# Attention stage: square roots of two batches in a row, with the batches written out and a lead of two

## The reference

```
Xn = layernorm(X);  P = Xn @ W_in.T + b_in      # 16 heads of 4 x 8: Q, K, V, G
sq   = |q|^2 + |k|^2 - 2 q.k                     # 256 x 256 for each head
dist = sqrt(max(sq, 0))
W    = (1e-4 + dist) ** -2;  W = W / (1e-4 + sum(W))
A = W @ V;  O = G * A;  X + O @ W_out.T + b_out
```

## Time and profile before

| | us |
|---|---|
| median of 3 runs | 1515.87 (1515.39 to 1519.79) |
| the profiled execution | 1515.65 |
| its span, first to last instruction | 1513.9 |
| attention stage in it, first score to last update | 816.4 to 1229.7 |

### The profile page before, as it was taken

One profiled execution on the slowest core, in us unless ns is written; L12 is line 12 of the kernel. 1 busy time (PEld: TensorE's weight loads), 2 busy tenths in 40 slices (PEclk: granted clock), 3 DMA queues, 4 the chain that ended last, 5 costly groups with the idle time before them and its releaser, 6 DMA issues. The chain is left out here.

```text
span 1513.9 us, 21515 instructions
## 1 busy us (share of the span) xinstructions
PE 1302.8 (86%) x6448; PEld 636.5 (42%) x6448; DVE 1271.4 (84%) x2150; ACT 1098.4 (73%) x1594; POOL 900.4 (59%) x1054
## 2 busy tenths in 40 slices
PE   4788888998997599999997787788888579999998
PEld 3344445544553244444442233333333234444443
DVE  3999999999999988888886888888878568888885
ACT  4677877786777456556653899999999956656564
POOL 5999889989988666665665232322222026656655
PEclk8999999999999999999998677867666689999999
DMA  7122113111311043322220000000000023333331
GB/s 252 57 73 95 56 56 102 65 56 56 111 56 57 10 166 144 131 112 112 112 112 0 1 1 0 0 0 0 0 0 1 1 113 120 120 119 119 146 155 61
DMA packets 27923, 111.54 MB, mean 74 GB/s; under 512 B 4049, under 2 KB 9570, under 8 KB 19426
## 3 DMA queue, kind: packets, MB, share of 16 engines
q1 hardware_dynamic: 27010, 110.21, 19.4%
q10 hardware_dynamic: 864, 0.74, 0.2%
HBM read 108.06 MB, written 2.88 MB: 73 GB/s over the span
## 5 line engine op out<-in xcount | busy, mean ns | idle before, releaser
L1042 POOL TENSOR_TENSOR e_h_lo<-e_h,e_h_hi 128x512 f16<-128x512 f32 x272 | 314.7, 1158 | 246.4 <-ACT e_h_hi L1124 233.6
L275 POOL TENSOR_TENSOR m_h<-m_b_sb,m_dx 128x512 f32<-128x512 f32 x256 | 347.0, 1383 | 45.6 <-POOLq L67 35.8
L690 DVE TENSOR_TENSOR_SCAN m_h<-m_decay,m_h 128x1024 f32<-128x1024 f32 x112 | 255.9, 2285 | 10.9 <-DVEq L60 7.5
L393 PE MATMUL m_y_ps<-m_hc,ident 128*128 128x512 f32 x512 | 251.1, 614 | 0.0
L528 ACT ACTIVATE m_decay<-m_delta,mw_a_log 128x255 f32<-128x255 f32 x448 | 185.1, 461 | 87.7 <-DVEq L695 87.5
L1119 ACT ACTIVATE e_g<-e_g 128x512 f32<-128x512 f32 x256 | 148.9, 582 | 122.7 <-PE e_g L1064 121.5
L1124 ACT ACTIVATE e_h_hi<-e_h 128x512 f16<-128x512 f32 x272 | 169.7, 624 | 84.6 <-DVE e_h L1175 82.9
L1621 DVE TENSOR_SCALAR a_d<-a_s 128x512 f32<-128x512 f32 x256 | 170.3, 687 | 54.9 <-PE a_s L1508 35.9
L1064 PE MATMUL e_g<-ef_x_hi,ew_gate_up 128*128 128x512 f16 x544 | 207.3, 381 | 4.7 <-PEq L103 3.2
L1069 PE MATMUL e_y<-e_h_hi,ew_down 128*128 128x512 f16 x544 | 205.9, 379 | 2.1 <-POOL e_h_lo L1042 2.1
L1064 PE MATMUL e_u<-ef_x_hi,ew_gate_up 128*128 128x512 f16 x544 | 207.4, 381 | 0.0
(11 more groups left out here) (236 smaller groups left out, 2080.4 us busy)
## 6 DMA issues: line engine op xcount, KB each, us to landing
e_c_rest<-mix SPq DMA_DIRECT2D x48, 1024.0 KB, 8.7
m_b_sb<-b_rows SPq DMA_DIRECT2D x64, 512.0 KB, 5.4
ef_c_head<-mix SPq DMA_DIRECT2D x16, 1024.0 KB, 4.6
ew_gate_up<-w_gate_up SPq DMA_DIRECT2D x1, 2176.0 KB, 13.9
out<-x_sb SPq DMA_DIRECT2D x8, 256.0 KB, 2.3
ew_down<-w_down SPq DMA_DIRECT2D x1, 1088.0 KB, 11.1
mw_conv_rows<-w_conv_rows ACTq DMA_DIRECT2D x1, 640.0 KB
mix<-ef_cT SPq DMA_DIRECT2D x16, 32.0 KB, 1.6
```

Of the source, the lines that this page charges most:

```text
L275: ins = nc.gpsimd.tensor_tensor(h[:, m % 4, :, c], b_sb[:, p, 2 * m:2 * m + 2], dx[:, p, c:c + 1].to_broadcast([P, 2, T]), ALU.mult)
L393: ins = nc.tensor.matmul(y_ps[:], ident[:], hc[:, m % 2, n].rearrange("p c t -> p (c t)"), start=(m == 0 and n == 0), stop=(m == PAIRS - 1 ...
L690: nc.vector.tensor_tensor_scan(flat, decay_of(m, p)[:], flat, 0.0, ALU.mult, ALU.add).then_inc(scan_chain, 1)
L1042: nc.gpsimd.tensor_tensor(h_lo[:, k], h[:, k], h_hi[:, k], ALU.subtract).then_inc(h_lo_ready, 1)
```

## The change

The distances now run two batches ahead (`LEAD = 2`): step b makes the distances of batch b+2 and the front part of batch b+3, and still weighs batch b. `d` gets a third buffer, and so does `gate`. All steps are written out, from -2 to 15. On ACT, batches 0 and 15 have their square roots alone; for the pairs (1, 2) to (13, 14) the odd step takes the square roots of both, waits for all six, loads the other table once, and the even step has logarithms and exponentials only. Step -2 (`opening`) runs all 16 distances of batch 0 first, and the front part of batch 1 behind them. V is freed by a signal of its own (`v_free`), given after `read_av`, in place of `gate_free`.

```diff
+        BUFS, LEAD = 3, 2
-        gate = sb("gate", [P, 2, TT, W])
-        d = sb("d", [P, 2, NH, TT * T])
+        gate = sb("gate", [P, BUFS, TT, W])
+        d = sb("d", [P, BUFS, NH, TT * T])
-        def batches(eng, body, prologue, epilogue):
-            prologue()
-            body(-1, 1, core=False, tail=False)
-            body(0, 0, tail=False)
-            with eng.Fori(0, NB // 2 - 2) as i:
-                body(i * 2 + 1, 1)
-                body(i * 2 + 2, 0)
-            body(NB - 3, 1, further=False)
-            body(NB - 2, 0, further=False, ahead=False)
-            body(NB - 1, 1, further=False, ahead=False, heads=False, last=True)
+        def batches(eng, body, epilogue):
+            def run(b):
+                body(b, b % 2, b % BUFS, b % 2 == 1, opening=b == -LEAD, core=b >= 0, tail=b >= 1, keeps=-1 <= b < NB - 1,
+                     heads=b < NB - LEAD, ahead=b < NB - LEAD - 1, further=b < NB - LEAD - 2, single=b in (0, NB - 1), last=b == NB - 1)
+            for n in range(-LEAD, NB):
+                run(n)
             epilogue()
...
         @block.gpsimd
+                if opening:
+                    front.norm(pool)
                 if ahead:
-                    front.residual(pool, b + 2)
+                    front.residual(pool, b + LEAD + 1)
+                if b >= 2:
+                    take(pool, gate_free)
                 if tail:
-                    take(pool, gate_free)
-                if heads:
-                    keep(1 - p)
+                    take(pool, v_free)
+                if keeps:
+                    keep(1 - p, (k + 1) % BUFS)
                 if ahead:
-                    front.pack(pool, p)
+                    front.pack(pool, 1 - p)
...
         @block.tensor
-                        score(h, 1 - p, not core)
+                        score(h, p, opening)
-                    if h == 1 and ahead:
-                        front.transpose_z(pe, t_ps[0])
+                    if h == (15 if opening else 1) and ahead:
+                        front.transpose_z(pe, t_ps[0])
-                    if h == 8 and ahead:
+                    if h == (15 if opening else 8) and ahead:
                         front.project(pe, t_ps)
...
         @block.scalar
+                def root(buffer):
+                    for first, n in ((0, 8), (8, 4), (12, 4)):
+                        take(act, d_ready)
+                        nc.scalar.activation(heads_of(buffer, first, n), heads_of(buffer, first, n), ACT.Sqrt).then_inc(root_chain, 1)
                 if not core:
                     return
-                for first, n in ((0, 8), (8, 4), (12, 4)):
-                    take(act, d_ready)
-                    nc.scalar.activation(heads_of(first, n), heads_of(first, n), ACT.Sqrt).then_inc(act_chain, 1)
-                nc.scalar.preload_act_table_set("natural_log_exp_and_others")
+                if single or paired:
+                    root(k)
+                    if not single:
+                        root((k + 1) % BUFS)
+                    act.wait_ge(root_chain, 3 if single else 6)
+                    act.sem_inc(root_chain, -3 if single else -6)
+                    nc.scalar.preload_act_table_set("natural_log_exp_and_others")
                 for half in range(2):
-                    act.wait_ge(act_chain, 1 + 2 * half)
...
         @block.vector
-                        distance(h, 1 - p)
-                    if h == 0 and ahead:
-                        front.normalise(dve, b + 2)
+                        distance(h, (k + LEAD) % BUFS)
+                    if h == (15 if opening else 0) and ahead:
+                        front.normalise(dve, b + LEAD + 1)
                     if h == 2 and tail:
                         read_av(0)
-                    if h == 2 and tail:
                         read_av(1)
+                        dve.sem_inc(v_free, 1)
-                    if h == 7 and core:
+                    if h == 7 and keeps:
                         take(dve, gate_ready)
...   # read_zT, read_qkvg, split_qk, statistics: at head 15 in the opening step, as before otherwise
```

More of the change, by code:

```diff
@@ L1473, in _, with keep, body @@
         def _(pool):
-            def keep(p):
+            def keep(p, k):
                 nc.gpsimd.tensor_scalar(v[:, p, :, :, 0:DH], front.by_head(p, 2), 1.0, 1.0, ALU.mult, ALU.mult).then_inc(v_ready, 1)
[L1477 to L1482, removed]
+                nc.gpsimd.tensor_scalar(gate[:, k], qkvg[:, p, :, 3 * W:4 * W], 1.0, 1.0, ALU.mult, ALU.mult).then_inc(gate_ready, 1)
+            def body(b, p, k, paired, opening, core, tail, keeps, heads, ahead, further, single, last):
                 if last:
                     experts.norm(pool)
+                if opening:
+                    front.norm(pool)
                 if ahead:
-                    front.residual(pool, b + 2)
+                    front.residual(pool, b + LEAD + 1)
+                if b >= 2:
+                    take(pool, gate_free)
                 if tail:
-                    take(pool, gate_free)
-                if heads:
-                    keep(1 - p)
+                    take(pool, v_free)
+                if keeps:
+                    keep(1 - p, (k + 1) % BUFS)
                 if ahead:
-                    front.pack(pool, p)
+                    front.pack(pool, 1 - p)
                 if further:
                     front.norm(pool)
-            batches(pool, body, prologue, lambda: None)
+                if last:
+                    take(pool, gate_free)
+            batches(pool, body, lambda: None)
         @block.tensor
@@ L1538, in project_out, with body @@
                 ins.then_inc(y_ready, 1)
-            def body(b, p, core=True, tail=True, heads=True, ahead=True, further=True, last=False):
+            def body(b, p, k, paired, opening, core, tail, keeps, heads, ahead, further, single, last):
                 for h in range(NH):
@@ L1572, in body @@
                             weights.wait(g, not tail)
-                            weigh(g, p)
+                            weigh(g, p, k)
                 if heads:
-                    scores_read.end(not core, False)
+                    scores_read.end(opening, False)
                 if core:
-                    weights.end(not tail, not heads)
+                    weights.end(not tail, last)
             def epilogue():
                 weights.wait(HG - 1)
-                weigh(HG - 1, 1)
+                weigh(HG - 1, (NB - 1) % 2, (NB - 1) % BUFS)
                 transpose_av()
@@ L1584, in epilogue, with body, heads_of @@
                 project_out()
-            batches(pe, body, lambda: None, epilogue)
+            batches(pe, body, epilogue)
         @block.scalar
         def _(act):
-            def body(b, p, core=True, tail=True, heads=True, ahead=True, further=True, last=False):
-                def heads_of(first, n):
-                    return d[:, p, first:first + n].rearrange("p h k -> p (h k)")
+            def body(b, p, k, paired, opening, core, tail, keeps, heads, ahead, further, single, last):
+                def heads_of(buffer, first, n):
+                    return d[:, buffer, first:first + n].rearrange("p h k -> p (h k)")
+                def root(buffer):
+                    for first, n in ((0, 8), (8, 4), (12, 4)):
+                        take(act, d_ready)
+                        nc.scalar.activation(heads_of(buffer, first, n), heads_of(buffer, first, n), ACT.Sqrt).then_inc(root_chain, 1)
                 if not core:
                     return
-                for first, n in ((0, 8), (8, 4), (12, 4)):
-                    take(act, d_ready)
-                    nc.scalar.activation(heads_of(first, n), heads_of(first, n), ACT.Sqrt).then_inc(act_chain, 1)
-                nc.scalar.preload_act_table_set("natural_log_exp_and_others")
+                if single or paired:
[5 more added lines that the diff above has]
+                    nc.scalar.preload_act_table_set("natural_log_exp_and_others")
                 for half in range(2):
-                    act.wait_ge(act_chain, 1 + 2 * half)
-                    nc.scalar.activation(heads_of(8 * half, 8), heads_of(8 * half, 8), ACT.Ln, bias=near[:, 0:1]).then_inc(act_chain, 1)
+                    nc.scalar.activation(heads_of(k, 8 * half, 8), heads_of(k, 8 * half, 8), ACT.Ln, bias=near[:, 0:1]).then_inc(act_chain, 1)
                 if last:
```

44 lines of the change are left out of this document (22 added, 22 removed).

## The result

The changed kernel takes 1525.87 us, median of five runs (1521.71 to 1527.30); five runs of the kernel before give 1518.63. The ratio is 1.0047 with an interval of 1.0036 to 1.0058: slower, by 7.2 us, and outside the 0.3% that can be told from no change. The profiled execution has 1526.83.

What follows compares the result with a forecast made beforehand. ACT bound the kernel at 24.35 us a batch, the PE and DVE loop close behind at 23.65. Opening, short steps, twelve steps and the last pair put batch 15's load at 1201.8 against 1196.95: +4.9 on 1515.65, 1520.5, range 1511 to 1527.

Steps and rivals of the forecast that it cites:

- own range: The total time if the forecast's own mechanism holds: 1516 to 1525 us.
- The forecast's mechanism: In attention, ACT stops being the bound and the loop of PE and DVE sets the pace; +4.9 us, chance 0.65.
- rival A: PE never held by ACT keeps 2.4 GHz, steps fall towards 21.9 us, ACT binds again: 1513.4 or 1510.5; chance 0.20.
- B: Rival: PE stays at 1.2 GHz more, steps settle at 24.2 us, the sum grows by 6.6 to 1527; chance 0.10.
- C: Rival: each batch still gets its two table loads on ACT, a pair costs 48.7 us: +13, 1529; chance 0.05.
- Table loads: On ACT, 18 loads in place of 32, 23.05 us a batch; only 0.70 of 1.30 per batch can come out.
- The new wait: On ACT, the wait for all six square roots ahead of the load: 0.1 us, nine times, hidden by idle time.
- Three buffers and own signal, written-out steps: Buffers of `d` and `gate`, V's signal and the unrolled loop: costed at nothing, within 0.1 us a step.
- Opening: Batch 1's front part stands alone behind batch 0's distances; batch 1's first distance comes at 844.0, 3.7 us later.
- Two short steps: Steps making batches 1 and 2, without a tail: 21.5 and 22.0 us; batch 3's first distance 2.3 late.
- Twelve steps at 23.65: Steps of the PE and DVE loop for batches 3 to 14: 283.8 us, batch 15's first distance at 1171.3.
- From the last distance of batch 14 to batch 15's load: On ACT, a whole pair behind that distance: 32.7 us, load at 1201.8 where before it stood at 1196.95.

Runs made afterwards that it cites:

- run 4: The changed kernel with one more table load on ACT ahead of each pair's square roots and batch 15's, eight in all: 1525.41 us, 1.0050.
- run 7: The changed kernel with four idle matmuls a step and one more table load for each of the seven pairs, batch 15 left out: 1523.12 us, 1.0032.
- run 2: The kernel before with its loop over pairs of batches written out, nothing else: 1518.81 us, 1.0005.
- run 3: The changed kernel with the signal that frees V given behind the norm and gate again: 1526.14 us, 1.0053.
- run 5: The changed kernel with four idle PE matmuls a step, behind the scores of heads 2, 3, 5 and 6, opening excepted: 1516.51 us, 0.9994.
- run 6: The kernel before with four idle PE matmuls a step: 1518.89 us, 1.0003.
- run 8: The changed kernel with batch 1's front part spread over the opening step and four idle matmuls in every step that makes a batch: 1514.36 us, 0.9971.
- run 9: The changed kernel with spread opening, idle matmuls only in steps with a tail, and pairs (0, 1) to (14, 15), 16 loads: 1512.40 us, 0.9966.

## Why the prediction came out right

The forecast said 1520.5 and slower by 4.9; it is slower by 7.2, inside the range of 1511 to 1527. In absolute time the 1525.87 lies 0.9 above the own range of 1516 to 1525, because five runs of the kernel before give 1518.63 where the three of the forecast gave 1515.87; that it stayed under 1527 is partly luck. Put on the forecast's base, 1515.65 + 7.2 = 1522.9 lies inside the own range. The forecast's mechanism happened, and neither rival A nor B nor C did.

Where the 7.4 us of the stage come from can be read off the two traces at three points: the first distance of batch 3, the first distance of batch 15, and the load ahead of batch 15's square roots. In the trace of before, DVE has the first distance of batch 15 here:

```profile
1175.40 2.02 DVE L1621 TENSOR_SCALAR a_d<-a_s 128x512 f32<-128x512 f32 x3 [1.35 <-PE a_s L1508]
```

Up to the first point the changed kernel loses 3.0 us (890.9 - 819.7 against 885.2 - 817.0: 4.1 more in the opening, 1.2 less in the two short steps). Over the twelve steps it gains 4.5 (285.7 against 1175.40 - 885.25 = 290.15, since before ACT held the later ones). From there to the load it loses 8.9 (1206.96 - 1176.53 = 30.43 against 1196.95 - 1175.40 = 21.55: a whole pair stands behind its last distance). Behind the load nothing changes. So the largest loss is the pair at the end; no run took that out by itself. Point by point:

- **Table loads**: 18 forecast, 9 + 9 counted. That only a part could come out because ACT stops being the bound: idle ahead of the second batch's last square root forecast at 1.2 us a pair, 1.25 to 1.99 found; ACT's idle time between batch 0's exponentials and batch 2's last square root forecast at some 25 us, 24.1 found; PE late, and not waiting up to batch 14 (the forecast had it so for every step). Runs 4 and 7 show it from both sides. The new wait, taken at 0.1, has 0.11.
- **Three buffers and own signal, written-out steps**, taken at nothing: runs 2 and 3 bear out the written-out steps and the signal. The third buffer was not tried alone.
- **Opening**: first distance of batch 1 27.0 us behind that of batch 0 forecast (844.0 - 817.02), 27.39 found. The sixteen distances were 0.3 short: they took 11.5 us, where the sum had 11.2 (its 10.0 without the hand-overs doesn't follow from 2.08 for three, which gives 11.1). The front part behind them was 0.1 short.
- **Two short steps**: 21.5 and 22.0 forecast, 21.7 and 22.1 in the stretches.
- **Twelve steps at 23.65**: this is the term that was mis-sized. They took 23.80, 12 x 0.15 = +1.8 us. I had averaged six steps of before, whose first two, of 22.9 and 23.4, belonged to a loop not yet settled; the other four have 23.87 to 23.88. The second of the six:

```profile
885.20:908.60 23.40, 19.68 (x138) 8.26 (x140) 20.10 (x45) 23.34 (x12) 7.38 (x18) 0.71 0.00 1
```

  Left alone, the loop settles at 23.86; the row to take was the one at 956.3.
- **From the last distance of batch 14 to batch 15's load**: 32.7 forecast. That distance is the second of the two at 1173.07, done at 1174.35; the load at 1206.96 is 32.6 later.

Together +2.5 us (1.8 in the steps, 0.7 in the opening and the short steps) of the 7.4 in the stage were not in the sum. The sign was right; the loss came out half as large again. The forecast's +4.9 lay on the bound of what can be told, which is why "within 0.3%" had 0.30 of the chance; with the missing 2.5 the time stands clear of it.

Rival A named the right lever and the wrong cause. The step does fall below 23.05 once PE's clock holds (run 5), but freeing PE from ACT doesn't hold it: the clock stayed at 0.79 in steps in which PE waited for ACT not once. For the price of a step the forecast's argument against A, the row from 956.3, was the better guide.

That the loads' gain is real and only covered is shown by the two edits together. The stage against that of the kernel before: matmuls alone +0.8 us (run 6), change alone +7.4, both -0.7 (run 5), both with the opening spread -2.9 (run 8), pairs from batch 0 -4.2 (run 9). By the medians runs 5 and 6 can't be told apart (0.9994 and 1.0003, their intervals overlap); run 8 can from run 6 (0.9971 and 1.0003), and run 7 against run 5 gives the price of the loads.

Still open is why the step without added matmuls settles at 23.86, why the one at 885.2 was shorter at a lower mean clock (23.4 at 0.71; the mean doesn't say which work fell into the slow part), and how few matmuls would hold the clock; one set of four was tried.

## What to carry to other kernels

Before taking work off the engine that is always busy, measure the period of the next loop: here the lag of PE behind ACT showed, in the trace of before, that it was only half a microsecond shorter. A gain that a second loop covers comes out when both are shortened, so test the two edits together before dropping either. And grouping work to save a switch puts a whole group behind the last input, which is paid once at the end (8.9 us here, read from the traces), and whatever is taken out from between other work in an opening is paid there in full.

## What the hardware showed that I had not expected

- **More work on PE made a step shorter.** Four matmuls, read by nobody (52 of the 60 took 0.39 us, the others 0.61), took a step from 23.86 to 23.02 on average, as the granted clock went from 0.79 to between 0.78 and 0.92. Without them the clock fell to 0.50, which is 1.2 GHz, after PE's waits between scores, and the transposes (1.94 against 1.06) and the projection (3.78 against 1.98) ran at that level.
- **It depends on the step.** In the steps without a tail the clock stayed low (0.50 and 0.61 in run 5, 0.50 and 0.59 in the change) and the same matmuls only cost: 22.46 and 22.69 in run 5 where the change has 21.69 and 22.09.
- **A loop of two engines settles.** Undisturbed, steps repeat at 23.86 for over 200 us, with one of 24.07 among them; with the matmuls they scatter between 22.0 and 24.4.
